# Local attention: the output product of the tile three back, issued between the queries' and the keys' projection instead of behind the turned queries

## The chip, the cores and the metric

One core of one Trainium2 chip runs the whole kernel. The metric is the device time of one execution in microseconds. It is given as the median of several runs. A difference under about 0.2% can't be told from none in this kernel.

## The reference, cut to what matters

The network has several stages in a row (tiled attention, causal attention with a convolution, a mixture of experts, a second causal attention) and then six layers, each of a local attention and a feed-forward part. The change lies in the local attention alone. There the input has 4 batches of 1024 tokens of 128 features, 16 heads of 64 and a window of 32 tokens:

```python
def local_attention(q, k, v):
    ...
    sim = jnp.einsum('bhwie,bhwje->bhwij', bq, bk2) * QK_SCALE
    sim = jnp.where(mask, -jnp.finfo(sim.dtype).max, sim)
    attn = jax.nn.softmax(sim, -1)
    out = jnp.einsum('bhwij,bhwje->bhwie', attn, bv2)
    return out.reshape(b, h, n, d)

def attn_layer(x, Wqkv, qs, ksc, Wo):
    b, n, _ = x.shape
    qkv = x @ Wqkv
    q, k, v = jnp.split(qkv, 3, -1)
    ...
    q = l2norm(q) * qs
    k = l2norm(k) * ksc
    ...
    out = local_attention(q, k, v)
    out = out.transpose(0, 2, 1, 3).reshape(b, n, INNER)
    return out @ Wo
```

Every window of 32 queries sees its own 32 keys and the 32 before them. The queries and keys are normalised by their length and turned by a rotary table. The last line, `out @ Wo`, is the product that the change moves.

## The kernel before, in words

The 4096 tokens of a layer are 32 tiles of 128 (`NT`). `local_attention` is a software pipeline over them, written by hand: each engine has one queue, and the helper `steps` issues, for step n = 0 to 34, the listed operations of tile n minus a lateness. An engine executes its own queue in the order written and waits on semaphores that the other engines raise. The function runs once per layer, six times in all, in a loop on the device, with all engines meeting at its end.

The PE queue of step n holds, before the change:

- `make_q(n)` (L1334): the projection of the queries, 128x1024, into the two PSUM banks of the score slot. It waits until `shift` has read the scores of tile n-2.
- `make_k(n)` (L1344): the projection of the keys into the two banks of the key slot. It waits for `o_out`, raised when ACT's `out_o` (L1470) of tile n-3 has copied the heads' outputs out of that slot.
- `turn_q(n-1)` (L1352): eight transposes of the scaled queries into the value slot. It waits for POOL's scaled queries.
- `project(n-3)` (L1429): the output product, eight fp32 products of 128x128 accumulated in the out slot. It waits for the same `o_out` of tile n-3 as `make_k(n)`, and for `added`, raised by DVE's `add` of the tile before it.
- `turn_k(n-1)` (L1363): eight transposes of the scaled keys into the score slot. It waits for POOL's scaled keys and for DVE's reading of the new queries.
- `turn_p(n-2)` (L1374): eight transposes of the probabilities into the value slot. It waits for `q_out`, because ACT's `out_q(n-1)` (L1455) must have read the turned queries out of that slot.
- `score(n-1)` (L1381 and L1390): first the mask band, two bf16 products that wait for ACT's `out_k(n-1)` (L1460), then the scores.
- `make_v(n)` (L1401): the values' projection into the value slot, after ACT's `out_p(n-2)` (L1465).
- `weigh(n-2)` (L1420): probabilities by values, into the key slot.

The ACT queue of a step is `square_q(n)` (L1442), `square_k(n)` (L1446, waits for `make_k(n)`), `out_q(n-1)` (L1455, waits for `turn_q`), `out_k(n-1)` (L1460, waits for `turn_k`), `out_p(n-2)` (L1465, waits for `turn_p`), `roots(n)` (L1450), `out_v(n)` (L1481, waits for `make_v`), `raise_p(n-1)` (L1474, the exponential, with a table load ahead of it) and `out_o(n-2)` (L1470).

The DVE queue is `rotate_q(n)` (L1495, L1498), `lengths(n)` (L1509 for queries, L1511 for keys; L1511 waits for `square_k`), `rotate_k(n)`, `maxima(n-1)` (L1516, waits for the scores), `shift(n-1)` (L1521), `invert(n)`, `add(n-3)` (L1548, waits for `project`), `totals(n-1)` (L1535, waits for the exponential) and `even(n-1)` (L1543). POOL adds the two rotary parts (L1561) and scales them (L1568). SP issues the copies of the values to the other half of the partitions (L1315 to L1320).

Of the kernel before, what the change touches and what calls it, by code (L numbers as in the profile page):

```python
# [1243 lines left out]
def local_attention(nc, ps, k, w, xs, cur, fetches):  # L1244
# [14 lines left out]
    with Stage(nc, "local") as st:  # L1259
# [36 lines left out]
        def steps(*plan):  # L1296
            for n in range(NT + AHEAD_TILES):
                for do, late in plan:
                    if 0 <= n - late < NT:
                        do(n - late)  # L1300

        with nc.Block() as block:
# [24 lines left out]
            def _(pe):  # L1327
# [97 lines left out]
                def project(t):  # L1425
                    pe.wait_ge(o_out, t + 1)
                    wait_past(pe, added, t)
                    for p in range(PAIRS):
# [2 lines left out]
                    last.then_inc(projected, 1)  # L1431

                pe.wait_ge(cleared, 2)
                steps((make_q, 0), (make_k, 0), (turn_q, 1), (project, 3), (turn_k, 1), (turn_p, 2), (score, 1),
                      (make_v, 0), (weigh, 2))

            @block.scalar
# [589 lines left out]
```

## Time and profile before

| | |
|---|---|
| median of 3 runs | 5512.2 us (5506.12 to 5514.61) |
| the profiled execution | 5511.92 us, of which the span from first to last instruction is 5510.1 us |
| mean granted TensorE clock | 0.946 of full speed |
| busy shares of the span | PE 87%, weight loads 52%, DVE 68%, ACT 59%, POOL 38% |

Times in the rows are microseconds from the start of the span. PE is TensorE's matmuls, PEld its weight loads (which overlap the matmuls), DVE VectorE, ACT ScalarE, POOL GpSimd. L1429 is line 1429 of the kernel. A bracket behind a row is the idle time of that engine just before it and what ended it. The start of a matmul is recorded and its end is modelled, so this text measures PE from start to start. Local attention runs in six stretches between about 1940 and 5410 us; each is 35 steps.

### The profile page before, as it was taken

How to read it: one execution, taken by the hardware profiler on the slowest of the kernel's cores; microseconds unless marked ns; L12 is line 12 of the kernel's file. 1: busy time of each engine (PE TensorE's matmuls, PEld its weight loads, DVE VectorE, ACT ScalarE, POOL GpSimd, SP SyncE). 2: the span in 40 equal slices, each digit the busy share in tenths (PEclk: the TensorE clock that was granted, in tenths of full speed). 3: DMA queues.
4: the chain of work that ended last, by engine and by line, in shares of the span. 5: the costliest groups of instructions: out<-in, count | busy, mean ns of one | idle time of the engine just before them, and what ended most of it. 6: DMA issues, size and time to landing. Idle time of an engine off the chain costs nothing. (4 is left out here: it accounts for less than half of the span.)

```text
span 5510.1 us, 168359 instructions
## 1 busy us (share of the span) xinstructions
PE 4792.3 (87%) x74640; PEld 2851.7 (52%) x74640; DVE 3755.1 (68%) x4672; ACT 3227.6 (59%) x3967; POOL 2068.5 (38%) x1534
## 2 busy tenths in 40 slices
PE   8768887996888689988999799988998899889997
PEld 5523334443333256654666366655665466646664
DVE  5567773332777478865887488847886688758885
ACT  5426664223566567665776477746776577647774
POOL 2430000004000055544555355525554455535552
PEclk9879998997899899999999899989999999989998
DMA  0021111001111111111111111101111111111111
GB/s 21 11 64 35 41 35 32 0 0 55 33 35 35 41 48 37 37 48 25 37 38 36 36 38 40 37 32 39 39 37 44 29 37 37 40 33 37 38 40 44
DMA packets 96366, 196.22 MB, mean 36 GB/s; under 512 B 27152, under 2 KB 45712, under 8 KB 93584
## 3 DMA queue, kind: packets, MB, share of 16 engines
q1 hardware_dynamic: 95632, 185.30, 13.1%
q8 instruction: 599, 9.81, 0.8%
q14 instruction: 135, 1.11, 0.1%
HBM read 63.57 MB, written 15.73 MB: 14 GB/s over the span
## 5 line engine op out<-in xcount | busy, mean ns | idle before, releaser
L1561 POOL TENSOR_TENSOR part_of_local<-part_of_local,sine_of_local 128x512 f32<-128x512 f32 x768 | 960.4, 1272 | 1074.4 <-DVE sine_of_local L1498 1074.4
L960 ACT ACTIVATE prob_of_ca<-ps 128x1024 f32<-128x1024 f32 (+3 forms) x768 | 596.5, 813 | 331.0 <-PE ps L834 228.8
L1568 POOL TENSOR_TENSOR part_of_local<-part_of_local,inverse_of_local 128x1024 f32<-128x1024 f32 x384 | 722.1, 1901 | 142.9 <-DVE inverse_of_local L1530 142.9
L1535 DVE TENSOR_REDUCE total_of_local<-prob_of_local 128x16 f32<-128x1024 f32 x192 | 234.3, 1220 | 422.1 <-ACT prob_of_local L1474 422.1
L1495 DVE TENSOR_TENSOR part_of_local<-ps,rope 128x1024 f32<-128x1024 f32 x384 | 466.5, 1215 | 58.4 <-ACT square_of_local L1442 58.4
L852 PE MATMUL ps<-keys_of_ca,queries_of_ca 64*128 64x512 bf16 (+3 forms) x1536 | 335.4, 346 | 182.0 <-DVE top_of_ca L992 69.6
L1498 DVE TENSOR_TENSOR sine_of_local<-ps,rope 128x1024 f32<-128x1024 f32 x384 | 466.2, 1214 | 0.0
L1344 PE MATMUL ps<-qkv,shifted 128*128 128x512 f32 x768 | 380.8, 618 | 78.7 <-ACT heads_out_of_local L1470 64.8
L1334 PE MATMUL ps<-qkv,shifted 128*128 128x512 f32 x768 | 392.9, 634 | 57.4 <-issue 33.8
L1420 PEld LDWEIGHTS ps<-prob_t_of_local,mixed_of_local 64*64 64x64 f32 x12288 | 339.0, 135 | 168.5 <-issue 158.7
L1420 PE MATMUL ps<-prob_t_of_local,mixed_of_local 64*64 64x32 f32 x12288 | 388.4, 221 | 17.3 <-issue 10.3
L1429 PE MATMUL ps<-heads_out_of_local,wo 128*128 128x128 f32 x3072 | 386.9, 281 | 14.1 <-ACT heads_out_of_local L1470 13.6
L992 DVE TENSOR_REDUCE top_of_ca<-ps 128x2 f32<-128x1024 f32 (+1 forms) x320 | 357.1, 1116 | 52.4 <-PE ps L834 25.7
L1420 PE MATMUL ps<-prob_t_of_local,values_of_local 64*64 64x32 f32 x12288 | 385.8, 220 | 5.8 <-issue 5.1
L1460 ACT ACTIVATE keys_of_local<-ps 128x1024 f32<-128x1024 f32 x192 | 196.6, 1024 | 323.6 <-PE ps L1363 323.6
L1401 PE MATMUL ps<-qkv,shifted 128*64 128x512 f32 x1536 | 378.5, 608 | 0.0
L1481 ACT ACTIVATE values_of_local<-ps 128x1024 f32<-128x1024 f32 x192 | 196.4, 1023 | 309.3 <-PE ps L1401 309.3
L1429 PEld LDWEIGHTS ps<-heads_out_of_local,wo 128*128 128x128 f32 x3072 | 368.2, 197 | 16.9 <-ACT heads_out_of_local L1470 16.9
L1420 PEld LDWEIGHTS ps<-prob_t_of_local,values_of_local 64*64 64x64 f32 x12288 | 341.6, 136 | 7.9 <-issue 6.8
L903 PE MATMUL ps<-prob_of_ca,values_of_ca 128*32 128x512 f32 (+3 forms) x3072 | 335.4, 509 | 0.6 <-ACT summed_of_ca L946 0.4
L792 POOL COPY values_of_ca<-vtok 128x256 f32<-128x256 f32 x32 | 12.7, 400 | 826.8 <-PE ps L903 826.6
L1446 ACT ACTIVATE square_of_local<-ps 128x1024 f32<-128x1024 f32 x192 | 196.6, 1024 | 215.2 <-PE ps L1344 214.9
(207 smaller groups left out, 10082.7 us busy)
## 6 DMA issues: line engine op xcount, KB each, us to landing
mixed_of_local<-values_of_local SPq DMA_DIRECT2D x636, 128.0 KB
mixed_of_local<-values_of_local SPq DMA_DIRECT2D x264, 64.0 KB
queries_of_ca<-q_parts SPq DMA_DIRECT2D x384, 32.0 KB
keys_of_ca<-k_parts SPq DMA_DIRECT2D x384, 32.0 KB
qkv<-in_qkv SPq DMA_DIRECT2D x7, 1536.0 KB, 6.4
rope<-in_rope SPq DMA_DIRECT2D x7, 1024.0 KB, 8.8
q_parts<-parts_of_ci SPq DMA_DIRECT2D x16, 384.0 KB, 2.6
k_parts<-parts_of_ci SPq DMA_DIRECT2D x16, 384.0 KB, 2.5
```

Source lines behind the costliest of these rows:

```text
L852: last = nc.tensor.matmul(place_of(n, pieces, width), queries[half_of(h), h // 2, qt * P:(qt + 1) * P], keys[half_of(h), h // 2, lo:lo + w ...
L960: nc.scalar.activation(prob[:, i % 2, 2 * two:2 * two + 2, j:], ps[:, 2 * two:2 * two + 2, j:], ACT.Exp, scale=scale).then_inc(raised, 1)
L992: nc.vector.reduce_max(to, pair[:, :, 0:width], AX_X).then_inc(pair_used, 1)
L1334: last = nc.tensor.matmul(two_banks(SCORE_SLOT)[:, a, :], xs[:, tokens(t)], w["qkv"][:, 0, chunk(a)], start=True, stop=True)
L1344: last = nc.tensor.matmul(two_banks(KEY_SLOT)[:, a, :], xs[:, tokens(t)], w["qkv"][:, 1, chunk(a)], start=True, stop=True)
L1401: last = nc.tensor.matmul(two_banks(VALUE_SLOT)[h * DH:(h + 1) * DH, a, :], xs[:, t * P + a * DH:t * P + (a + 1) * DH], w["qkv"][:, 2, chu ...
L1420: last = nc.tensor.matmul(out, src[rows, t % RING * 2 + i // 2, p + e, :], prob_t[rows, p + e, i * WIN:(i + 1) * WIN], start=True, stop=True)
L1429: last = nc.tensor.matmul(two_banks(OUT_SLOT)[:, 0, 0:P], w["o"][:, p, :], heads_out[:, p, :], start=p == 0, stop=p == PAIRS - 1)
L1495: nc.vector.tensor_tensor(part[:, t % 2, side], by_head(slot), table(2 * side, t), ALU.mult).then_inc(parts, 1)
L1498: nc.vector.tensor_tensor(sine[:, side], by_head(slot), table(2 * side + 1, t), ALU.mult).then_inc(parts, 1)
L1561: nc.gpsimd.tensor_tensor(out, out, sine[:, side, :, (1 - to) * half:(2 - to) * half], ALU.add).then_inc(rotated, 1)
L1568: nc.gpsimd.tensor_tensor(part[:, t % 2, side], part[:, t % 2, side], by, ALU.mult).then_inc(scaled, 1)
```

## The change

The PE queue's plan is reordered: `project` with lateness 3 moves from behind `turn_q` to between `make_q` and `make_k`. Nothing else is touched: the operations, their operands and their semaphores are the same, and no other queue changes.

```diff
                 pe.wait_ge(cleared, 2)
-                steps((make_q, 0), (make_k, 0), (turn_q, 1), (project, 3), (turn_k, 1), (turn_p, 2), (score, 1),
+                steps((make_q, 0), (project, 3), (make_k, 0), (turn_q, 1), (turn_k, 1), (turn_p, 2), (score, 1),
                       (make_v, 0), (weigh, 2))
```

## Rows read from the trace of the kernel before

**Rows 1.** The page: its head and its busy times by engine.
```profile
span 5510.1 us, 168359 instructions
...
PE 4792.3 (87%) x74640; PEld 2851.7 (52%) x74640; DVE 3755.1 (68%) x4672; ACT 3227.6 (59%) x3967; POOL 2068.5 (38%) x1534
```

**Rows 2.** Windows, 300 us inside layer 3: busy time of each engine, PEclk, DMA.
```profile
core 0: us, PE busy (x) PEld busy (x) DVE busy (x) ACT busy (x) POOL busy (x), PEclk, DMA share, GB/s
3200.00:3500.00 300.00, 286.90 (x6322) 196.14 (x6315) 250.29 (x280) 213.45 (x222) 176.85 (x121) 1.00 0.17 38
```

**Rows 3.** Waits over all local attention: us in total, times, longest.
```profile
PEld ps L1344 <- ACT heads_out_of_local L1470: 205.1, 174, 1.3
...
PEld ps L1381 <- ACT keys_of_local L1460: 95.1, 186, 1.5
```

**Rows 4.** Timeline, PE, one step: start us, us long, engine and line.
```profile
3319.92 1.98 PE L1334 MATMUL ps<-qkv,shifted 128*128 128x512 f32 x4
...
3322.39 1.98 PE L1344 MATMUL ps<-qkv,shifted 128*128 128x512 f32 x4 [0.48 <-ACT heads_out_of_local L1470]
...
3324.21 1.04 PE L1352 MATMUL ps<-sb_ident,part_of_local 128*128 128x128 f32 x8
...
3325.08 1.95 PE L1429 MATMUL ps<-heads_out_of_local,wo 128*128 128x128 f32 x16
...
3326.87 1.04 PE L1363 MATMUL ps<-sb_ident,part_of_local 128*128 128x128 f32 x8
...
3327.74 1.04 PE L1374 MATMUL ps<-sb_ident,prob_of_local 128*128 128x128 f32 x8
...
3329.02 0.60 PE L1381 MATMUL ps<-band,sb_ident_b 128*128 128x512 bf16 x2 [0.24 <-ACT keys_of_local L1460]
...
3330.97 1.94 PE L1401 MATMUL ps<-qkv,shifted 128*64 128x512 f32 x8
```

**Rows 5.** Timeline, ACT, the same step and the end of the one before.
```profile
3318.03 1.02 ACT L1481 ACTIVATE values_of_local<-ps 128x1024 f32<-128x1024 f32 x1 [1.53 <-PE ps L1401]
...
3319.07 1.28 ACT L1474 ACT_TABLE_LOAD   x1
...
3320.36 1.06 ACT L1474 ACTIVATE prob_of_local<-prob_of_local 128x1024 f32<-128x1024 f32 x1
...
3321.33 1.00 ACT L1470 ACTIVATE heads_out_of_local<-ps 128x1024 f32<-128x1024 f32 x1
...
3324.41 1.02 ACT L1446 ACTIVATE square_of_local<-ps 128x1024 f32<-128x1024 f32 x1 [1.16 <-PE ps L1344]
...
3325.33 1.02 ACT L1455 ACTIVATE queries_of_local<-ps 128x1024 f32<-128x1024 f32 x1
...
3327.94 1.02 ACT L1460 ACTIVATE keys_of_local<-ps 128x1024 f32<-128x1024 f32 x1 [1.59 <-PE ps L1363]
```

**Rows 6.** Timeline, DVE and POOL, around the same step.
```profile
3316.15 1.23 DVE L1516 TENSOR_REDUCE top_of_local<-ps 128x16 f32<-128x1024 f32 x1
...
3317.41 1.23 DVE L1521 TENSOR_TENSOR prob_of_local<-ps,top_of_local 128x1024 f32<-128x1024 f32 x1
...
3319.26 3.76 POOL L1568 TENSOR_TENSOR part_of_local<-part_of_local,inverse_of_local 128x1024 f32<-128x1024 f32 x2 [0.61 <-DVE inverse_of_local L1530]
...
3321.46 1.22 DVE L1535 TENSOR_REDUCE total_of_local<-prob_of_local 128x16 f32<-128x1024 f32 x1 [2.20 <-ACT prob_of_local L1474]
...
3327.53 1.21 DVE L1511 TENSOR_REDUCE length_of_local<-square_of_local 128x16 f32<-128x1024 f32 x1
...
3331.08 1.23 DVE L1516 TENSOR_REDUCE top_of_local<-ps 128x16 f32<-128x1024 f32 x1
```

**Rows 7.** Timeline, PE, the first step after the last tile, layer 3.
```profile
3605.97 1.09 PE L1352 MATMUL ps<-sb_ident,part_of_local 128*128 128x128 f32 x8 [1.23 <-POOL part_of_local L1568]
...
3607.14 2.05 PE L1429 MATMUL ps<-heads_out_of_local,wo 128*128 128x128 f32 x16
...
3609.03 1.04 PE L1363 MATMUL ps<-sb_ident,part_of_local 128*128 128x128 f32 x8
```

## The prediction

> **What bounds the kernel now.** The page comes first: PE is busy for 87% of the span and no other engine for more than 68% [rows 1]. That is an average, so the table of windows is read next, for 300 us inside one layer's local attention: PE is busy for 287 of them, DVE for 250, and the clock is granted in full [rows 2]. The reader is to see that neither engine is quite full, so a ring of waits sets the pace. The timeline of one step shows it. The maxima of two neighbouring tiles start at 3316.15 and 3331.08 [rows 6], so a step lasts 14.93 us.
>
> Follow what each operation waited for, with no gap on the way. The values' projection starts at 3330.97 and, one step earlier, 14.93 before that, at 3316.04 [rows 4]; ACT copies it at 3318.03, then loads the exponential's table, takes the exponential, and copies the heads' outputs at 3321.33 [rows 5]. That copy releases `make_k` at 3322.39; then PE runs `make_k`, `turn_q`, `project` and `turn_k` back to back until 3326.87 and later [rows 4]. ACT has idled for the turned keys, copies them at 3327.94 [rows 5], and this releases the band at 3329.02, after which the scores run until the values' projection of 3330.97 [rows 4]. The ring has closed and holds no slack. The list of waits says that it does so everywhere: `make_k` waited for the heads' outputs 174 times, which is 29 steps in each of 6 layers, and the band for the copied keys 186 times [rows 3].
>
> Two things lie beside the ring. `turn_p` starts at 3327.74 and is hidden by the copy of the keys [rows 4, 5]. DVE's `shift` ends at 3318.64, while the table load behind the copied values starts at 3319.07: DVE has 0.43 us to spare [rows 5, 6].
>
> **The change part by part.** One call moves on one queue. `project` issues matmuls only, no DMA, so the queues of SP and POOL are not passed; it is moved ahead of `make_k` and `turn_q` on PE. It waits for the same copy of the heads' outputs that `make_k` waits for, so it can't use the 0.48 us in which PE idles there [rows 4]: the idle time only moves ahead of `project`. Its second wait, for `added`, is for a sum one step old and costs nothing.
>
> Before, from the release to `turn_k` PE needs 3326.87 - 3322.39 = 4.48: `make_k` 1.82, `turn_q` 0.87, `project` 1.79, each from start to start [rows 4]. The same three still stand before `turn_k`, so to a first look nothing changes. What changes is what lies between `make_k` and `turn_k`, and that is ACT's work.
>
> - `project` after a wait has a row: in the emptying pipeline it starts at 3607.14 and its successor at 3609.03, 1.89 [rows 7]; run on without a wait it takes 1.79 [rows 4]. So `make_k` starts at 3324.18 to 3324.28 where it started at 3322.39.
> - `square_k` starts 2.02 after `make_k`: at 3326.20 to 3326.30, before at 3324.41 [rows 4, 5].
> - `out_q` follows on ACT by 0.92, as 3325.33 - 3324.41 [rows 5]: at 3327.12 to 3327.22. Its input is ready by 1.82 + 1.07 after `make_k` (1.07 is `turn_k` to its copy), 3327.07 to 3327.17, so ACT's queue decides, narrowly. `out_q` loses 1.8 us, since the long gap of ACT ahead of the keys' copy was where it fitted.
> - `out_k` follows by another 0.92: at 3328.04 to 3328.14, where it was at 3327.94 and waited for nothing but PE. It is 0.10 to 0.20 late.
> - `turn_p` needs the value slot, which `out_q` frees. A copy releases PE 1.08 after its start (3327.94 to 3329.02) [rows 4, 5], so `turn_p` starts at 3328.20 to 3328.30, not 3327.74. It is no longer hidden. After it the band can start 0.87 later at the earliest, and 0.10 more if a block that had to wait costs that again, as `project` shows. This gives 3329.07 to 3329.27.
> - The band therefore starts at the later of two: by the keys' copy at 3329.12 to 3329.22, by `turn_p` at 3329.07 to 3329.27. Against 3329.02 that is 0.10 to 0.25 late. I take 0.18, the middle: the 0.10 of a restart has a row and should come once, while the two ways of counting `project` differ by as much.
>
> Everything behind the band is as before, and the ring has no slack, so the step becomes 14.93 + 0.18 = 15.11. What else could be late? DVE's second length reduction starts at 3327.53 [rows 6] and needs `square_k`, which now ends at 3327.22 to 3327.32: hidden by 0.2, and DVE's spare 0.43 lies behind that. `make_v` waits for the copied probabilities, which come by 3328.30 + 1.07 + 1.08 = 3330.45, still 0.7 ahead of it. The scaled queries and keys come from POOL between 3319.26 and 3323.02 [rows 6], before either turn. `add` gets its product earlier, which nobody waits for.
>
> Steps concerned: `project` and `make_k` share a step for n = 3 to 31, 29 steps, times 6 layers: 174. 174 x 0.18 = 31.3 us; by the ends 17.4 and 43.5.
>
> The emptying pipeline adds a little. In step 32 there is no `make_k`; before, `turn_q` ran at 3605.97, ahead of the wait for the heads' outputs, and `project` at 3607.14 [rows 7]. Now `turn_q` stands behind `project`: it starts at 3609.03 and `turn_k` at 3609.90 in place of 3609.03. The last tile's scores are 0.87 us late, with nothing beside them: taken as 0.9 with the later `turn_p`, 6 x 0.9 = 5.4 us.
>
> Sum: 31.3 + 5.4 = 36.7 us on the profiled execution of 5511.9 (span 5510.1 and 1.8 around it) gives 5548.6, say 5549. The median of the runs, 5512.2, is 0.3 above the profiled one, which is no difference here. The ends are 5534 and 5561.
>
> **The rivals.**
>
> *No change.* If DVE's ring were the true bound, 0.1 to 0.2 us on PE's would vanish. For it: `maxima` starts at 3331.08 without an idle moment before it, so DVE is ready at the same time as the scores, and it is busy 83% of the window. Against it: 2.20 us of idle time ahead of the sums in each step [rows 6], and the spare 0.43. It would give 5512, or 5517 with the emptying. The Trainium skill (Perfetto Trace Analysis, Identifying the Most-Contended Engine) says that matmul occupancy is a poor measure and weight-load occupancy a good one; by that rule PE at 196 of 300 us has room, DVE is the engine that counts, and the order on PE should be free: 5512. The trace speaks against it, by 174 waits for ACT at one place.
>
> *Faster.* The place is the stretch from the release to `make_k`, which holds `project` alone. The price is 174 times what it falls short. The break-even: the band starts 4.99 after `make_k` (2.02 + 0.92 + 1.08 + 0.87 + 0.10), and must start before 3329.02, so `make_k` must start before 3324.03, 1.64 after the release. At 1.50 it would be -0.14 x 174 + 5.4 = -19, or 5493. For it: `project` stood between transposes of another shape and its loads may run closer with a projection behind it. Against it: both rows have it at 1.79 or more, 0.112 for each of 16 passes [rows 4, 7]. The Trainium skill (TensorE: Matmul & The Clock Gate, Back-to-back issue gap) gives about 81 ns for a load and matmul of 128 columns in a stream; by that figure `project` would need 16 x 0.081 = 1.3 and the step would shrink by an estimated 0.35. The trace's 0.112 speaks against it.
>
> *Slower by more.* PE now stops twice, before `project` and before `turn_p`, and the band comes right behind the second stop. If that stop costs 0.2 or more beyond its length (loads that used to run ahead), a step loses 0.35: 174 x 0.35 + 5.4 = 66, or 5578. The granted clock belongs here too: it is full in this window with a stop of 0.48 in each step [rows 2, 4], and the new stops are no longer than that.
>
> *The change doesn't do what it says:* not possible here, the order on PE is the whole of it.
>
> **How the numbers follow.** About 0.2% (11 us) is what a measurement can tell from no change. Forecast, 5534 to 5561: 0.68. No change: 0.10. Faster: 0.06. Slower by more, 5561 to 5590: 0.10. Slower by less than the ends, 5523 to 5534: 0.06. So slower 0.84, same 0.10, faster 0.06. The range leaves out the first two rivals and the far part of the third: 5525 to 5570.
>
> **What would show it.** In the changed kernel's timeline: a step of 15.0 to 15.2; `square_k`, `out_q` and `out_k` back to back on ACT, so that the gap before `out_k` (1.59 before, [rows 5]) is gone and the one before `square_k` has grown to about 3.0; an idle moment of PE ahead of `turn_p` with ACT's queries as its releaser; `project` in place of `make_k` as the waiter for the heads' outputs, 174 times; the band's wait for the keys shrunk to nearly nothing. I am wrong if the step is still 14.93, which means that the band was not on the ring, or if `make_k` follows `project` by less than 1.64.

## The result, and the profile after

| | median | ratio to before, 95% interval |
|---|---|---|
| before | 5512.8 us (5506.1 to 5514.6, 4 runs) | |
| changed kernel | 5594.0 us (5587.9 to 5597.9, 4 runs) | 1.0148 (1.0131 to 1.0166) |

The change makes the kernel 81 us slower. The prediction had 37 us slower, 5549 us, with a range of 5525 to 5570. The page of the changed kernel, head, busy times and the queue that fetches instructions:

```profile
span 5589.2 us, 168167 instructions
...
PE 4806.3 (86%) x74448; PEld 2878.3 (51%) x74640; DVE 3754.5 (67%) x4672; ACT 3229.0 (58%) x3967; POOL 2068.5 (37%) x1534
...
q8 instruction: 599, 9.81, 0.7%
```

No engine works appreciably more than before [rows 1]; the span has grown by waiting. The list of waits over all local attention (us in total, times, longest):

```profile
ACT square_of_local L1446 <- PE ps L1344: 527.0, 186, 3.0
...
PEld ps L1429 <- ACT heads_out_of_local L1470: 231.4, 191, 2.5
...
DVE top_of_local L1516 <- PE ps L1390: 154.8, 191, 8.1
...
PEld ps L1390 <- issue: 115.6, 229, 1.4
PEld ps L1374 <- issue: 103.9, 179, 0.6
```

Three of these lines are new or grown. `project` in place of `make_k` now waits for the heads' outputs. ACT idles 527 us ahead of `square_k`, and hardly at all ahead of the keys' copy, where each step had 1.59 [rows 5]. And DVE's `maxima` waits 154.8 us for the scores, where it was 64.2. The line `PEld ps L1374 <- issue`, 179 times, is the new stop ahead of the probabilities' transposes.

One undisturbed step of the changed kernel, PE and then ACT, to be laid beside [rows 4, 5]:

```profile
3343.78 2.05 PE L1429 MATMUL ps<-heads_out_of_local,wo 128*128 128x128 f32 x16 [0.49 <-ACT heads_out_of_local L1470]
...
3345.67 1.88 PE L1344 MATMUL ps<-qkv,shifted 128*128 128x512 f32 x4
...
3347.39 1.04 PE L1352 MATMUL ps<-sb_ident,part_of_local 128*128 128x128 f32 x8
...
3348.26 1.04 PE L1363 MATMUL ps<-sb_ident,part_of_local 128*128 128x128 f32 x8
...
3349.68 1.06 PE L1374 MATMUL ps<-sb_ident,prob_of_local 128*128 128x128 f32 x8 [0.38 <-ACT queries_of_local L1455]
...
3351.10 1.48 PE L1390 MATMUL ps<-keys_of_local,queries_of_local 64*32 64x64 f32 x128
...
3352.52 1.94 PE L1401 MATMUL ps<-qkv,shifted 128*64 128x512 f32 x8
```

```profile
3342.72 1.01 ACT L1470 ACTIVATE heads_out_of_local<-ps 128x1024 f32<-128x1024 f32 x1
...
3347.59 1.03 ACT L1446 ACTIVATE square_of_local<-ps 128x1024 f32<-128x1024 f32 x1 [2.95 <-PE ps L1344]
...
3348.51 1.03 ACT L1455 ACTIVATE queries_of_local<-ps 128x1024 f32<-128x1024 f32 x1
...
3349.41 1.04 ACT L1460 ACTIVATE keys_of_local<-ps 128x1024 f32<-128x1024 f32 x1
...
3350.78 1.03 ACT L1465 ACTIVATE prob_t_of_local<-ps 128x1024 f32<-128x1024 f32 x1 [0.33 <-PE ps L1374]
```

From `project` to `make_k` 1.89 us, to `turn_q` 1.72, to `turn_k` 0.87: the stretch of PE is as long as before, 4.48. ACT's three copies follow back to back. `turn_p` starts 1.42 after `turn_k` and no longer 0.87, `make_v` comes 8.74 after the release where it came 8.58 in [rows 4]. The step lasts 15.08 us in place of 14.93.

But not every step is such a step. From one `maxima` to the next, the first two left out, 5 to 10 steps of a layer last over 15.5 us (up to 17.9), where the kernel before has at most one such (16.1). Here is one of them, PE and the first DVE operation that waits, layer 3, step 20:

```profile
3471.18 1.06 PE L1374 MATMUL ps<-sb_ident,prob_of_local 128*128 128x128 f32 x8 [0.38 <-ACT queries_of_local L1455]
...
3472.30 0.38 PE L1381 MATMUL ps<-band,sb_ident_b 128*128 128x512 bf16 x1
...
3472.61 1.35 PE L1390 MATMUL ps<-keys_of_local,queries_of_local 64*32 64x64 f32 x113
...
3474.48 0.34 PE L1390 MATMUL ps<-keys_of_local,queries_of_local 64*32 64x64 f32 x15 [0.52 <-issue]
...
3474.75 1.94 PE L1401 MATMUL ps<-qkv,shifted 128*64 128x512 f32 x8
3474.92 1.23 DVE L1516 TENSOR_REDUCE top_of_local<-ps 128x16 f32<-128x1024 f32 x1 [1.01 <-PE ps L1390]
```

The 128 recorded matmuls of the score block are torn into 113 and 15, with 0.5 us of idle PE between them (0.74 from start to start, where 0.01 is usual). Such a gap inside a block is called a tear below, and its size is given from start to start. The same block of the kernel before, step 20 of the same layer, is whole:

```profile
3432.22 1.04 PE L1374 MATMUL ps<-sb_ident,prob_of_local 128*128 128x128 f32 x8
...
3433.50 0.61 PE L1381 MATMUL ps<-band,sb_ident_b 128*128 128x512 bf16 x2 [0.24 <-ACT keys_of_local L1460]
...
3434.04 1.49 PE L1390 MATMUL ps<-keys_of_local,queries_of_local 64*32 64x64 f32 x128
...
3435.45 1.08 PE L1401 MATMUL ps<-qkv,shifted 128*64 128x512 f32 x4
```

In the changed kernel 37 score blocks are torn, in the same steps of all six layers (3, 5, 20, 22 and 24 in every one, 14, 16 and 18 in some) and at the same matmul; the gaps add up to 35.0 us, 27.0 of them idle PE. In the kernel before no score block is torn.

The first squared queries of a layer follow those of the layer before it after 593.2 us before the change and 606.9 us after it, in the mean of five intervals. The 13.7 us are made up so: 29 steps of 0.15 are 4.4; torn blocks and what follows them another 6.3 in those steps; from the last squared queries to the next layer's first 3.5 (135.3 for 131.8); the first steps, in which the pipeline fills, are 0.6 to 0.7 shorter, for which I have no reason. Six times 13.7 is 82 us.

### The profile page after: what moved, and what is told of

It is laid out like the page before. It is cut to its first block and busy times, and to the rows that moved or that the text cites. A ratio compares the mean times of both kernels' runs of the same rounds, so it can differ in the third digit from the quotient of the medians.

```text
span 5589.2 us, 168167 instructions
## 1 busy us (share of the span) xinstructions
PE 4806.3 (86%) x74448; PEld 2878.3 (51%) x74640; DVE 3754.5 (67%) x4672; ACT 3229.0 (58%) x3967; POOL 2068.5 (37%) x1534
## 3 DMA queue, kind: packets, MB, share of 16 engines
q8 instruction: 599, 9.81, 0.7%
## 5 line engine op out<-in xcount | busy, mean ns | idle before, releaser
L1429 PE MATMUL ps<-heads_out_of_local,wo 128*128 128x128 f32 x3072 | 413.5, 291 | 90.2 <-ACT heads_out_of_local L1470 89.2
L1334 PE MATMUL ps<-qkv,shifted 128*128 128x512 f32 x768 | 394.4, 636 | 60.2 <-issue 33.8
L1344 PE MATMUL ps<-qkv,shifted 128*128 128x512 f32 x768 | 366.3, 600 | 11.0 <-DVE sine_of_local L1498 11.0
L1516 DVE TENSOR_REDUCE top_of_local<-ps 128x16 f32<-128x1024 f32 x192 | 235.2, 1225 | 154.8 <-PE ps L1390 154.8
L1390 PE MATMUL ps<-keys_of_local,queries_of_local 64*32 64x64 f32 x24576 | 295.2, 227 | 27.0 <-issue 27.0
```

Source lines behind the costliest of these rows:

```text
L1334: last = nc.tensor.matmul(two_banks(SCORE_SLOT)[:, a, :], xs[:, tokens(t)], w["qkv"][:, 0, chunk(a)], start=True, stop=True)
L1344: last = nc.tensor.matmul(two_banks(KEY_SLOT)[:, a, :], xs[:, tokens(t)], w["qkv"][:, 1, chunk(a)], start=True, stop=True)
L1429: last = nc.tensor.matmul(two_banks(OUT_SLOT)[:, 0, 0:P], w["o"][:, p, :], heads_out[:, p, :], start=p == 0, stop=p == PAIRS - 1)
```

## The experiments

Twelve more kernels ran. The names below are those of the PE plan; "emptying" is steps 32 to 34 of a layer, and the filled pipeline is the steps from 3 to 31.

**1 and 2. The change in the emptying alone, and in steps 0 to 31 alone.** A plan of its own for the emptying:

```diff
+                for do, late in (emptying if emptying and n >= NT else plan):
```

> The order of before in steps 0 to 31 and the changed order in steps 32 to 34 alone. My theory after seeing both traces: the changed kernel loses in three places, and this one is the emptying pipeline, where PE now idles 2.2 us ahead of the product, the granted clock falls to 1.2 GHz and the product and the turned queries take twice their time: about 3.6 us per layer, 6 x 3.6 = 22 us over before, ratio 1.004. The step of the filled pipeline stays at 14.93 and no score block is torn apart by a gap. Rival (my prediction's own term): only the 0.9 us of order, 5 us in all, ratio 1.001.

Measured: 5522.0 us, ratio 1.0014 (1.0004 to 1.0023), some 8 us. The 22 us did not come; my prediction's own 5 us lie in the interval. The clock did fall in five of the six layers and the band came at 21.7 us after the last squared queries for 19.1, but the last sum of a layer came 39.3 us after them for 37.9: later idle stretches, which cost the kernel before its clock as well, gave half of the delay back.

> The changed order in steps 0 to 31 and that of before in steps 32 to 34. Theory: a step of 15.08 (174 x 0.15 = 26 us) and some 37 torn score blocks of nearly 1 us each (35 us), together about 61 us over before, ratio 1.011; with the emptying-only kernel the two sum up to the change's 81 us. Rival: if the losses are not independent (the clock in the emptying follows from what the steps before did), the sum of the two kernels' losses misses 81 by over 15 us.

Measured: 5587.1 us, ratio 1.0131 (1.0114 to 1.0148), 72 us; a step of 15.08 and 36 torn score blocks with 37.0 us of gaps. The two losses sum up to 80 us of the 81. So nine tenths of the loss belong to the filled pipeline. The size I gave it, 61, was too small by 11: the end of its layers was slower too (133.4 us from the last squared queries to the next layer, for 131.8), although its emptying is that of before.

**3. A stop ahead of the probabilities' transposes, in the order of before.**

```diff
                         pe.wait_ge(q_out, t + 2)
+                        pe.wait_ge(k_out, t + 2)
```

> The order of before; the only edit is that the transposes of the probabilities also wait for the copied keys of the tile ahead, so PE stops ahead of them, as in the changed kernel, and the mask band follows behind them without a stop of its own. Theory (the score block is torn wherever a block of instructions ends in it and the sequencer has not had the time of a fetch since it passed the start of that block): the step is 14.93 + 0.98 = 15.9 (transposes 0.87 and a restart of 0.10 come onto the ring) and the scores are torn at the same places as in the changed kernel (before matmul 118 in step 3, 125 in step 5, 107 in step 18, and so on), with the order of before: over 25 tears, 5513 + 174 x 0.98 + 30 = 5714 us. Rival (the tears come with the moved product, through PSUM or the wait for the heads' outputs): no tears, 5684 us.

Measured: 5720.5 us (one run), a step of 15.90, and 25 torn score blocks, in steps 5, 20, 22 and 24 of all six layers and once in step 3. Layer 3, step 20, PE:

```profile
3523.44 1.06 PE L1375 MATMUL ps<-sb_ident,prob_of_local 128*128 128x128 f32 x8 [1.21 <-ACT keys_of_local L1461]
...
3524.86 1.35 PE L1391 MATMUL ps<-keys_of_local,queries_of_local 64*32 64x64 f32 x113
...
3527.00 0.34 PE L1391 MATMUL ps<-keys_of_local,queries_of_local 64*32 64x64 f32 x15 [0.79 <-issue]
```

`project` was not moved here, and the block of step 20 is torn at the same matmul, 113. The stop makes the tears; the product's place only makes the stop. In steps 3 and 18, which I had named too, all blocks but one stayed whole. Their number, 25 where I had said over 25, and the time, 5720 for 5714, fit all the same.

**4. More instructions ahead of the steps.** Waits that are long satisfied, once per layer in the changed kernel:

```diff
-                pe.wait_ge(cleared, 2)
+                for _ in range(9):
+                    pe.wait_ge(cleared, 2)
```

> The changed kernel with 8 more waits on PE, all satisfied already, once per layer ahead of step 0. In the changed kernel the gaps within the scores stand before the 107th, 114th, 121st and 128th of 128 recorded matmuls, two steps apart, each some 2.4 us after an instruction fetch of queue q8 began. Theory: they are the ends of blocks of instructions, so 8 more instructions move each of them 4 recorded matmuls (8 instructions, a load and a matmul each) to the front, to 102, 109, 116, 123 in the count of the same steps. Rival (they come from data, a bank or a semaphore): their places stay where they are. Time the same as the changed kernel's within 10 us in both.

Measured: the tears stand at 115 in step 3, 122 in step 5, 111 in step 20, 118 in 22 and 125 in 24, each 2 matmuls ahead of its old place and not 4. The page explains the half: 168383 instructions, 24 more than in the kernel before, so 8 waits per layer became 4 instructions, and a recorded matmul is two (its weight load and itself). The changed kernel's own count, 168167, can't be used here: 192 records of the mask band's first matmul are missing from its trace. Time 5609.1 us in the one run, 15 more than the changed kernel and outside what I had allowed.

With 49 waits in place of 9 (`range(49)` in the same line):

> The changed kernel with 48 more satisfied waits once per layer, which in the trial with 8 were issued in pairs: 24 more instructions. Theory (ends of instruction blocks): each tear moves 12 matmuls forward in its score block, to 105 in step 3, 112 in 5, 119 in 7, 126 in 9, and 101, 108, 115, 122 in steps 20 to 26, with an uncertain 94 in step 18; 8 to 9 tears per layer where there were 6, and about 0.9 us for each: 15 us more than the changed kernel, 5608 us, ratio to before 1.0175. Rival (the place does not matter to the time): 5595 us, ratio 1.015.

Measured: 5620.1 us, ratio 1.0202 (1.0186 to 1.0217). The tears stand at 105, 112, 119 and 126 in steps 3, 5, 7 and 9 and at 101, 108, 115 and 122 in steps 20 to 26: every place as forecast. Step 7 of layer 3, PE, with 119 matmuls ahead of the gap:

```profile
3273.34 1.06 PE L1374 MATMUL ps<-sb_ident,prob_of_local 128*128 128x128 f32 x8 [0.38 <-ACT queries_of_local L1456]
...
3274.76 1.40 PE L1390 MATMUL ps<-keys_of_local,queries_of_local 64*32 64x64 f32 x119
...
3276.82 0.32 PE L1390 MATMUL ps<-keys_of_local,queries_of_local 64*32 64x64 f32 x9 [0.65 <-issue]
```

But the number is 35 and not 50, since the steps at the edge (5, 20, 22) were torn in some layers only. So the added time does not come from more tears: 3.0 us of each layer lie between the last squared queries of one layer and the first of the next (138.3 for 135.3), the stretch in which the added waits themselves stand. That is 18 us in six layers, while the two medians are 26 apart; the rest is not accounted for. The place of a tear is shown to be a place in the instruction stream; what a shift of it is worth is not shown.

**5. What the tears wait for.** The trace has the packets of queue q8, 599 in all and 16 KB each (9.81 MB), the same number in both kernels. In the changed kernel one lies in the window of 3472.1 to 3472.3 us, inside the step shown above, and in the kernel before one in 3432.1 to 3432.3. The DMA view of these two windows, changed kernel first:

```profile
q8 instruction: 1, 0.02, 33.6%
```

```profile
q8 instruction: 1, 0.02, 41.4%
```

Their starts are 3472.16 and 3432.18. In the changed kernel the torn block goes on at 3474.48, 2.32 after the fetch began. Over all 37 tears this distance is 2.27 to 2.65 us, whatever the matmul. In 11 cases (steps 14, 16 and 18) the block stays whole at the same place, and there the fetch had begun 3.05 us or more before that matmul. In the kernel before, the fetch begins with `turn_p` at 3432.22, PE then stops for the keys' copy until 3433.50, and the 114th matmul is reached 2.98 us after the fetch began; in steps 3, 5, 20, 22 and 24 of the six layers it is 2.84 to 3.24 us at the places of the tears, twice less, 2.46 and 2.35, and in steps 14, 16 and 18 the fetch begins over 6 us ahead. There the fetch is always in time, though twice only just. In the changed kernel PE stops ahead of `turn_p` and not behind it, the fetch begins 0.98 us after `turn_p` starts, and only some 1.6 us are left to the same matmul. Of the 1.4 us that the fetch has lost here, the stop behind `turn_p` is the smaller part: the 114th matmul comes 2.54 us after `turn_p` starts and not 2.93, 0.39 sooner. The larger part is that the fetch begins later: 0.89 to 1.56 us after `turn_p` starts at the 37 tears, and 0.90 to 1.56 at the 25 tears of the late stop, where in the kernel before it begins within 0.3 us of it (28 of the 30 in steps 3, 5, 20, 22 and 24). A stop ahead of `turn_p` thus brings both. Why it delays the fetch is not shown; that the sequencer is held by the wait and reaches the end of its block later is my reading.

Two neighbouring tears are 7 matmuls apart in steps two apart, which is how the step's instructions fall against blocks of a fixed size. The Trainium skill (Runtime: NRT & Kernel Launch, Instruction fetch mechanics) says that an engine's instructions are refilled in blocks of 16 KiB, 256 instructions, by the sequencer's own DMA queue while it executes, and that crossing a block boundary is mostly hidden. The size of the packets agrees; hidden it is in the score blocks of the order of before, and in these 37 places it is not.

The kernel before is not free of such tears either. Of its 192 blocks of `weigh` 31 have a gap of over 0.25 us, 23 us in all, and each goes on 2.26 to 2.93 us after a packet of q8 began. The changed kernel has 33 of them with 24 us, so they are no part of the difference. Here is one in the kernel before, layer 3, step 26, after the 125th matmul:

```profile
3529.49 0.28 PE L1420 MATMUL ps<-prob_t_of_local,values_of_local 64*64 64x32 f32 x5
...
3530.56 0.30 PE L1420 MATMUL ps<-prob_t_of_local,values_of_local 64*64 64x32 f32 x3 [0.78 <-issue]
```

**6. Half of the product moved.** Four pairs of heads between `make_q` and `make_k`, four behind `turn_q`; the emptying of before.

```diff
-                steps((make_q, 0), (make_k, 0), (turn_q, 1), (project, 3), (turn_k, 1), (turn_p, 2), (score, 1),
+                steps((make_q, 0), (project_start, 3), (make_k, 0), (turn_q, 1), (project_rest, 3), (turn_k, 1),
...
```

> Half of the output product (4 of 8 pairs of heads) stands between the queries' and the keys' projection, the other half behind the turned queries; emptying as before. Theory of a threshold: the keys' projection is 0.9 us late and not 1.8, so the copied queries still free the value slot at about 3327.3 on the clock of [rows 4], before the probabilities' transposes want it at 3327.74; the whole loss in the filled pipeline vanishes: step 14.93, no torn score blocks, 5513 us, ratio 1.000 to 1.001. Rival (loss in proportion to the delay): half of some 60 us, ratio 1.005.

Measured: 5532.9 us, ratio 1.0041 (1.0028 to 1.0055). The undisturbed step is 14.93, so the threshold on the ring is right: 0.9 us of delay to `make_k` cost nothing there. But 16 score blocks are torn, by 0.47 us each, and 42 blocks of `weigh` where there were 31, with 10.7 us more of gaps in these. So the loss of the filled pipeline did not vanish, and the ratio came nearer to the rival's. The kernel has 168 instructions more than the one before (168527 for 168359), which is one for each of 28 steps in 6 layers; that it is the second half's own wait is my reading. Its blocks of instructions therefore end elsewhere, and a step as long as the old one can be torn at another place.

**7. The clock in the emptying.** What the changed kernel does after its last tile, PE, and the table of windows for that stretch:

```profile
3649.25 3.79 PE L1429 MATMUL ps<-heads_out_of_local,wo 128*128 128x128 f32 x16 [2.22 <-ACT heads_out_of_local L1470]
...
3652.83 1.92 PE L1352 MATMUL ps<-sb_ident,part_of_local 128*128 128x128 f32 x8
...
3654.54 1.30 PE L1363 MATMUL ps<-sb_ident,part_of_local 128*128 128x128 f32 x8
...
3657.18 0.38 PE L1381 MATMUL ps<-band,sb_ident_b 128*128 128x512 bf16 x1 [0.17 <-issue]
```

```profile
core 0: us, PE busy (x) PEld busy (x) DVE busy (x) ACT busy (x) POOL busy (x), PEclk, DMA share, GB/s
...
3648.60:3655.40 6.80, 6.15 (x30) 6.15 (x31) 2.42 (x3) 1.22 (x2) 1.28 (x1) 0.52 0.18 41
```

In [rows 7] `turn_q` ran ahead of `project`, which kept the idle time of PE short. Here PE idles 2.2 us, the granted clock is 0.52 in the window of 6.8 us that begins near the end of the stop, its level of 1.2 GHz, and the product takes 3.58 us from start to start, not 1.89. The stop is 2.1 to 2.4 us long in all six layers, and the clock falls in five of them; the band comes 22.1 to 23.3 us after the last squared queries in those, 20.5 in the sixth and 19.1 in all layers before the change. The Trainium skill (TensorE: Matmul & The Clock Gate, Terms) says that a monitor of PE's activity gates the clock, at half rate in one state. These rows agree: 0.52 behind the idle stretch. Products that nobody reads, into an unused PSUM bank, keep PE at work:

```diff
+                    if t == NT - 3:
+                        keep_busy(4)
```

> The changed kernel with four more 128x512 products per layer, into an unused PSUM bank and read by nobody, ahead of the output product of step 32, where PE otherwise idles for 2.2 us. Theory: the granted clock then does not fall there; the band of step 32 comes some 20.5 us after the last squared queries in all six layers (now 22.1 to 23.3 in five of them), about 2 us per layer and 12 us in all faster than the changed kernel, 5582 us, ratio to before 1.0125. Rival (the clock falls for another reason, such as the waits of the step before): no gain, 5594 us or more.

Measured: 5595.4 us, ratio 1.0156 (1.0142 to 1.0171). The clock did not fall there in any layer, but the band came at 21.4 to 21.7, since each added product takes two passes and the four of them last some 3.5 us and not 1.8. With `keep_busy(2)`:

> The changed kernel with two added products ahead of the output product of step 32 in place of four. The first trial kept the clock up in all six layers, but each added product takes two passes, 0.86 us, so that four outlasted the idle 2.2 us by more than a microsecond and gave the gain away. Two take 1.7 us and fit. Theory: no fall of the clock there, the band of step 32 comes 20.5 us after the last squared queries in all layers, 6 x 2 = 12 us less than the changed kernel: 5582 us, ratio to before 1.0125. Rival (the fall of the clock is only put off to the next idle stretch): the band is early, the end of the layer is not, and the time stays at 5594 us, ratio 1.0147.

Measured: 5587.6 us, ratio 1.0145 (1.0129 to 1.0160). Layer 3, PE, and the window that answers to the one above:

```profile
3645.05 2.05 PE L1436 MATMUL ps<-heads_out_of_local,wo 128*128 128x128 f32 x16 [0.49 <-ACT heads_out_of_local L1477]
...
3646.94 1.04 PE L1352 MATMUL ps<-sb_ident,part_of_local 128*128 128x128 f32 x8
...
3650.08 0.59 PE L1381 MATMUL ps<-band,sb_ident_b 128*128 128x512 bf16 x2
```

```profile
3643.80:3650.50 6.70, 5.88 (x44) 4.59 (x42) 2.70 (x3) 3.36 (x5) 1.88 (x2) 1.00 0.22 50
```

The clock is whole, `project` takes 1.89, and the band comes at 20.3 in all six layers. So the trace shows that the idle stretch costs the clock here. The gain in time is 6 us by the medians and 2 by the ratios, of the 12 us expected, and can't be told from none: the last sum of a layer comes 39.8 us after the last squared queries (mean of six), after 41.0 in the changed kernel and 37.9 before, because the clock falls later instead, as the rival said.

The same in the kernel before, twelve added products and then three:

```diff
+                    if t == NT - 1:
+                        keep_busy(3)
...
+                    if t == NT - 2:
+                        keep_busy(5)
+                    if t == NT - 1:
+                        keep_busy(4)
```

The first stands ahead of the last `weigh`, the other two ahead of the last two output products; in the second kernel they are none, 2 and 1.

> The order of before with idle PE time of the emptying pipeline filled in the same way: five such products ahead of the output product of step 33, three ahead of the last product of probabilities and values, four ahead of the last output product. If the clock is what makes these steps long (the output product takes 3.8 us there in place of 2.0), each layer gains 2 to 4 us: 5495 us, ratio 0.997. Rival (the clock falls all the same, as PE has idled before and after): nothing, or the fillers' own time lost, ratio 1.000 to 1.002.

Measured: 5544.9 us, ratio 1.0064 (1.0052 to 1.0076), slower than both theories had it: in five of the six layers the clock stayed up until the last sum, and the products, twice as long as reckoned, stood in the way.

> The order of before with two such products ahead of the output product of step 33 and one ahead of the last. Theory: the last sum of a layer comes some 36 us after the last squared queries in each layer, in place of 36.5 to 40.0; 6 x 1.8 = 11 us less than before: 5502 us, ratio 0.998. Rival (as in the trial with twelve: the fillers stand on the ring and cost their own time): 5513 to 5520 us, ratio 1.000 to 1.001.

Measured: 5507.2 us, ratio 0.9997 (0.9988 to 1.0006). No difference; in four of six layers the clock fell all the same.

**8. The ring shortened.** If the stop ahead of the band is part of the cover of the fetch, then an order that shortens the ring by way of that stop must pay for it. The last pairs of the product behind `turn_k`, in the kernel before:

```diff
-                steps((make_q, 0), (make_k, 0), (turn_q, 1), (project, 3), (turn_k, 1), (turn_p, 2), (score, 1),
+                steps((make_q, 0), (make_k, 0), (turn_q, 1), (project_start, 3), (turn_k, 1), (project_rest, 3),
...
```

> The order of before, but the last two of the product's eight pairs of heads stand behind the turned keys and not ahead of them. The keys' transposes then start when the rotated queries are read, about 3326.6 on the clock of [rows 4] in place of 3326.87; the band by the keys' copy at 3328.75; by PE (0.45 for two pairs, 0.87 for the probabilities' transposes, 0.10 if it restarts) at 3327.92 to 3328.02 and 3328.80 to 3328.90. So the ring is 0.1 to 0.2 shorter and a step 14.73 to 14.83: 17 to 35 us faster without tears, 5478 to 5496 us. But PE no longer stops ahead of the band, which is what gave the instruction fetch its time. Theory of the fetch: there are tears in the score blocks again, at some 0.9 us each, and they eat all or most of it: ratio 0.998 to 1.004. Rival (tears need the stop ahead of the transposes of the probabilities, which stays absent here): no tears, ratio 0.994 to 0.997.

Measured: 5507.8 us, ratio 0.9988 (0.9979 to 0.9996). The undisturbed step is 14.75 us, as reckoned. 23 score blocks are torn, by 0.40 us each where I had said 0.9, and 81 blocks of `weigh` (31 before), 35 us of gaps more in all. By some 6 us it is the only kernel of the study whose interval lies below the one before, and that is less than the 0.2% which the prediction calls a difference.

> The same with the last pair alone behind the turned keys. The keys' transposes start at 3326.65, the probabilities' at 3327.74 as before, and the band waits for the keys' copy until 3328.80: PE still stops ahead of it, for about 0.2 us, where it stopped 0.48. Step 14.93 - 0.22 = 14.71: without tears 38 us faster, 5475 us, ratio 0.993. Theory of the fetch: the cover between the probabilities' transposes and the end of the scores shrinks by 0.22, and in the order of before the nearest fetch landed 0.5 us before it was needed (2.84 to 3.2 us after its start, where 2.35 is the least), so few or no tears: ratio 0.993 to 0.996. Rival (any shortening of the stop tears the scores): 0.999 or more.

Measured: 5513.6 us, ratio 0.9997 (0.9987 to 1.0007). The undisturbed step is 14.72, as reckoned, but I had expected few tears and there are 37 score blocks torn by 0.41 us each, and 67 of `weigh`. One of the torn score blocks, layer 3, step 14, PE:

```profile
3344.33 1.06 PE L1363 MATMUL ps<-sb_ident,part_of_local 128*128 128x128 f32 x8
...
3345.23 0.39 PE L1429 MATMUL ps<-heads_out_of_local,wo 128*128 128x128 f32 x2
...
3345.45 1.04 PE L1374 MATMUL ps<-sb_ident,prob_of_local 128*128 128x128 f32 x8
...
3347.05 1.09 PE L1390 MATMUL ps<-keys_of_local,queries_of_local 64*32 64x64 f32 x86
...
3348.44 0.67 PE L1390 MATMUL ps<-keys_of_local,queries_of_local 64*32 64x64 f32 x42 [0.30 <-issue]
```

The stop ahead of the band in the order of before, which I put at 0.48, is 0.41: 3329.02 - 3327.74 is 1.28, of which the transposes take 0.87 [rows 4]. The keys' transposes now start when the rotated queries are read, `turn_p` right behind the last pair, and the block is torn after 86 matmuls, far from the place where the kernel before had little to spare. My count of the cover from `turn_p` to the end of the scores alone was too narrow. I take it that the time counts which PE spends over the whole block of 256 instructions, and that each order shifts it elsewhere; no run here tests this by itself.

## Why the prediction was wrong

- *What bounds the kernel, and the ring.* Right. The step's length followed from the ring within 0.03 us in five kernels: 15.08 in the changed one (15.11 predicted), 14.93 with half of the product moved, 15.90 with the late stop, 14.75 and 14.72 with the shortened ring.
- *The band, 0.10 to 0.25 late, taken as 0.18.* Right: 0.15. ACT's queue sets `out_q`, and the stop moves ahead of `turn_p`, as reckoned: 1.89, 1.72 and 0.87 on PE, `square_k`, `out_q` and `out_k` 0.92 and 0.90 apart. That is 26 us of the 81.
- *"Everything behind the band is as before, and the ring has no slack, so the step becomes 14.93 + 0.18."* This is the step that failed. Behind the band come the scores, 256 of the step's instructions within 1.3 us, and they had been whole only as long as PE stopped right ahead of them. That stop ahead of the band (0.41 us from start to start, 0.24 of them idle in [rows 4]), which the sum took for time that merely changes its place, was part of the time in which the next block of instructions arrived. Moved ahead of `turn_p`, the stop takes from the fetch at both ends: the same matmul is reached 0.39 us sooner after `turn_p`, and the fetch begins some 1.0 us later. So the fetch is no longer covered: 37 score blocks are torn, 35.0 us of gaps, in the place where the sum had nothing. The order of before with such a stop ahead of `turn_p`, and nothing else changed, tears 25 score blocks, at the same matmuls. Where the stop behind `turn_p` was shortened and none put ahead of it (experiment 8), the tears were 0.4 us and not 0.95.
- *The emptying, 0.9 us per layer.* This term was sized too small. From the last squared queries of a layer to the next layer's first the growth is 3.5 us, 21 us in all for the 5 reckoned. The order alone is about what was reckoned: with the change in the emptying alone this stretch grows by 0.7 us (132.5 for 131.8), and the band is 1.0 us late where the clock held. The clock was left out of the term. At its lower level it stands for 25.3 us of the stretch in the kernel before (mean of five), 24.5 with the change in the emptying alone, 28.4 with the change in the steps alone (which makes the stretch 133.4) and 31.2 in the changed kernel (135.3). So the growth goes along with the clock; why it is low for longer behind the changed steps I have not settled. The fall at each idle stretch also varies from layer to layer of one kernel.
- *The rivals.* "Slower by more" was right in its sign and its place, the second stop, at 66 us for 81, and by luck near in size: it had a restart of matmuls in mind, but an undisturbed step, with both stops in it, is only 0.15 longer and not 0.35. Its sentence on the clock looked at the filled pipeline alone, where it was right; in the emptying the stop is over four times longer. "No change" fell with the step; "faster" with `project` at 1.89 from start to start.
- *The range.* Built from the ring's terms alone, it ended where the unseen costs began. A bound for "a stop moves on an engine that issues hundreds of small instructions" was missing.

## What to carry to other kernels

An idle moment of an engine need not be lost: here a packet of instructions was on its way in it. Ahead of a dense block of small instructions, a short stop may help to hide the fetch of the next block of them. An order that removes the stop can pay with gaps inside that block, and one that puts it further ahead can pay more, since here the fetch then began later as well; look for a group whose matmuls are split by "issue" in the same steps of every layer. And where a stretch in a chain is emptied, see what the move does to the idle time ahead of it: here a stop of over 2 us cost the clock in five layers of six, and the stops of 0.5 us in every filled step did not.

## What the runs showed of the hardware that was not expected

- With a stop ahead of `turn_p` the packet of q8 began some 1.0 us later after its start than without.
- A torn score block of the changed kernel goes on 2.27 to 2.65 us after the packet on q8 began (37 tears), while the score block issues 256 instructions in 1.3 us. The score blocks of the kernel before reach these places 2.35 us or more after it, and none is torn.
- Two neighbouring waits came out as one instruction: 8 per layer added 24 instructions in six layers, not 48.
- The fall of the clock in a stop of 2.1 to 2.4 us came in five layers of six of the same kernel, and made the output product 3.58 us long in place of 1.89 in layer 3; with the stop filled it did not come there, but it came later, in all six layers.
